# Attention and mixture-of-experts layer: P turned in 32x32 blocks, PV in 32x64 tiles of TensorE

## The reference

```
x = x + attention(layernorm(x));  x = x + ffn(layernorm(x))
q, k, v = y @ W_q + b_q, y @ W_k + b_k, y @ W_v + b_v        # per head, 128 -> 64
P = softmax(causal(q k^T / 8));  z = P v;  out = sum over heads of z W_o, + b_o
```

## Time and profile before

| | us |
|---|---|
| median of 3 runs | 1330.94 (1328.23 to 1332.27) |
| the profiled execution: time | 1327.09 |
| its span | 1325.4 |
| TensorE busy (share) | 1259.4 (95%) |
| VectorE busy | 816.3 (62%) |
| ScalarE busy | 820.3 (62%) |
| GpSimd busy | 302.8 (23%) |

### The profile page before, as it was taken

How to read it: one execution, slowest core, us unless ns; L and a number is a source line. 1 busy time by engine, 2 the same in 40 slices (tenths; PEclk the granted TensorE clock), 3 DMA queues, 4 the chain that set the end, 5 groups by cost and what they waited for, 6 DMA issues and landing times.

```text
span 1325.4 us, 26554 instructions
## 1 busy us (share of the span) xinstructions
PE 1259.4 (95%) x7404; PEld 855.9 (65%) x7404; DVE 816.3 (62%) x2230; ACT 820.3 (62%) x1749; POOL 302.8 (23%) x311
## 2 busy tenths in 40 slices
PE   2899999999999999999999999999999997899995
PEld 1666666667666676676667777666777675445552
DVE  6666666666666666666666666666666676556563
ACT  3756666666666666666666666666666656476664
POOL 3322222222222222222222222222222201012323
PEclk8999999999999999999999999999999998999998
DMA  8866555555555555555555555555555551000000
GB/s 199 207 138 136 130 127 131 131 131 130 128 127 127 127 127 127 127 127 127 127 126 127 127 127 124 127 127 127 127 127 127 127 127 37 9 9 8 16 8 24
DMA packets 78983, 148.68 MB, mean 112 GB/s; under 512 B 41328, under 2 KB 52592, under 8 KB 67056
## 3 DMA queue, kind: packets, MB, share of 16 engines
q1 hardware_dynamic: 78960, 148.41, 49.0%
HBM read 43.21 MB, written 4.46 MB: 36 GB/s over the span
## 4 chain that ended last, share of the span: by engine, by line
PE 80%; DVE 6%; issue 5%; SPq 3%; ACT 2%; DMA 2%; POOL 1%; DVEq 0%; ACTq 0%; POOLq 0%
PE Z L517 19%; PE TB L504 15%; PE SPS L494 10%; PE SPS L495 8%; PE MB L480 8%; PE MB L525 4%; PE MB L485 4%; PE Z L641 2%; PE SPS L633 2%; DVE SSB L849 2%; PE TB L625 1%; PE MB L659 1%; SPq L367 1%; DVE ZN L798 1%; PE SPS L598 1%
## 5 line engine op out<-in xcount | busy, mean ns | idle before, releaser
L849 DVE CUSTOM_DVE_ANT_0 SSB<-SPS,MASK 128x640 f32<-128x640 f32 (+7 forms) x512 | 385.4, 753 | 311.2 <-PE SPS L495 302.7
L1115 ACT ACTIVATE PR<-SSB,NM 128x640 f32<-128x640 f32 (+7 forms) x512 | 394.3, 771 | 109.7 <-DVE NM L849 104.2
L504 PE MATMUL TB<-IDENT,PR 128*128 128x128 f32 x2304 | 349.9, 275 | 17.5 <-ACT PT L780 7.8
L504 PEld LDWEIGHTS TB<-IDENT,PR 128*128 128x128 f32 x2304 | 272.7, 141 | 102.2 <-issue 42.9
L780 ACT ACTIVATE PT<-TB 128x512 f32<-128x512 f32 (+3 forms) x384 | 205.0, 534 | 180.5 <-PE TB L504 180.5
L494 PE MATMUL SPS<-KH,QS 128*128 128x512 f32 (+2 forms) x768 | 313.7, 408 | 2.6 <-DVE NM L849 1.3
L517 PE MATMUL Z<-PT,V 128*64 128x512 f32 (+3 forms) x1536 | 269.3, 492 | 0.0
L495 PE MATMUL SPS<-KL,QS 128*128 128x512 f32 (+2 forms) x768 | 261.5, 348 | 0.0
L395 POOL CAST RH<-RAW 128x512 fp32r<-128x512 f32 x124 | 75.5, 609 | 772.0 <-ACT RAW L1077 769.1
L782 DVE COPY PT<-TB 128x128 f32<-128x128 f32 (+3 forms) x384 | 186.3, 485 | 76.2 <-PE TB L504 76.2
L517 PEld LDWEIGHTS Z<-PT,V 128*64 128x64 f32 x1536 | 101.7, 136 | 141.7 <-issue 132.3
(11 more groups left out here) (157 smaller groups left out, 880.3 us busy)
## 6 DMA issues: line engine op xcount, KB each, us to landing
KH<-RH SPq DMA_DIRECT2D x62, 512.0 KB, 8.6
KL<-RL SPq DMA_DIRECT2D x62, 512.0 KB, 9.1
XTB<-xt_scratch SPq DMA_DIRECT2D x32, 512.0 KB, 4.0
RSB<-rcp_scratch SPq DMA_DIRECT2D x128, 128.0 KB, 2.8
QS<-RH SPq DMA_DIRECT2D x31, 512.0 KB, 4.4
QS<-RL SPq DMA_DIRECT2D x31, 512.0 KB, 6.6
WQK<-in_W_q SPq DMA_DIRECT2D x33, 64.0 KB, 1.9
WQK<-in_W_k SPq DMA_DIRECT2D x33, 64.0 KB, 2.1
```

The source lines that it names most:

```text
L504: last = pe.transpose(TB[idx % 2][:, k * P:(k + 1) * P], PR[n % 4][:, (j0 + k) * P:(j0 + k + 1) * P], IDENT[:, :])
L849: v.tensor_tensor_reduce(out=SSB[n % 2][:, 0:w], in0=SP_[n % 2][:, 0:w], in1=MASK[:, S - w:S], scale=1.0, scalar=BIG, op0=ALU.add, op1=ALU ...
L1115: act.activation(PR[n % 4][:, 0:w], SSB[n % 2][:, 0:w], ACT.Exp, bias=NM[:, col:col + 1], scale=-1.0, accum_out=L[:, col:col + 1]).then_in ...
```

## The change

- TensorE turns nothing any more. VectorE turns the exponentials of a whole unit in 32x32 blocks with one instruction (`dve_turn`), from rings PRS and PRL into PTZ. Inside each block keys and queries are exchanged; which of the four 32-row groups a block lies in stays that of its queries.
- PV is therefore done in tiles of 32 rows by 64 columns: for each key tile kt, each 32-key block j, each row group i (the 32-query blocks) and each head h one matmul, with V's block j in the partitions of group i, and up to 4 x 32 queries streamed. Row group i writes to bank i of ZB. V is stored to DRAM and read back four times into VR, so that each partition group holds all of V.
- PV of both halves is done in the next step: the first half behind unit 3, the second half in one visit behind unit 6.
- TB, Z and MB are now the four banks of ZB, so projections, V, PV and output share them and wait for each other's evacuation.
- RH and RL are gone. GpSimd rounds and subtracts directly into QS, KH and KL, on half of the partitions each (two casts and two subtractions for each quarter), and only K is spread by DMA to the other half: four DMAs of 256 KB.
- ScalarE evacuates V (the bias of V is folded into b_o by `pe_bias`) and copies the output to OT; GpSimd adds OT to X (`add_out`).
- The FFN weights are issued before the sums of step 31.

```diff
+        def turned_block(g, h, kt, j, rows):
+            lo = max(kt - g * TC, 0)
+            key = slice(kt * P + j * TR, kt * P + (j + 1) * TR)
+            step = PT_ROW[g] + h * P
+            c0 = PT_BASE[g] + h * PT_LEAD[g]
+            tiles = PTZ[rows, c0:c0 + TC * step].rearrange("p (r c) -> p r c", c=step)
+            if h == 0:
+                return tiles[:, lo:TC, key]
+            return tiles[:, 0:TC - lo, key][:, ::-1, :]
...
-        def pe_values(pe, it, par, g, j):
...
-            for h in range(2):
-                last = pe.matmul(Z[h * DH:(h + 1) * DH, off:CH], V[par][:, j, h * DH:(h + 1) * DH], PT[g][:, h, j, off:CH],
-                                 start=(j == 0), stop=(j == nj - 1))
+        def pe_values(pe, it, g, blocks):
+            for kt in blocks:
...
+                c0 = g * P + max(kt - g * TC, 0) * TR
+                for j in range(P // TR):
+                    for i in range(P // TR):
+                        rows = slice(i * TR, (i + 1) * TR)
+                        for h in range(2):
+                            last = pe.matmul(ZB[h * DH:(h + 1) * DH, i, c0:(g + 1) * P], VR[rows, j, kt, h * DH:(h + 1) * DH],
+                                             turned_block(g, h, kt, j, rows), start=(kt == 0 and j == 0),
+                                             stop=(kt == (g + 1) * TC - 1 and j == P // TR - 1))
...
+        def spread_v(sp, it, half, par):
+            sp.wait_ge(v_stored[par], (half + 1) * DMA)
+            wait(sp, pv_done[1], it)
+            src = v_dram[par].rearrange("(j k) (t c) -> k j t c", k=TR, c=P)
+            for tiles, landed in ((slice(0, TC), v_early), (slice(TC, QT), v_late)):
+                for i in range(P // TR):
+                    sp.dma_start(VR[i * TR:(i + 1) * TR, :, tiles, :], src[:, :, tiles, :]).then_inc(landed, DMA)
...
+            v.transpose(turned_of(n), exps_of(n)).then_inc(turned, 1)
...
+            gp.tensor_tensor(QS[par][DH:P, h, part], q, q_high.bitcast(F32), ALU.subtract).then_inc(split_done, 1)
+            gp.tensor_tensor(KL[par][DH:P, h, part], k, k_high.bitcast(F32), ALU.subtract).then_inc(split_done, 1)
...
+            scores(2, 3)
+            values(0, 0, 1, 2, 3)
+            scores(4, 5, 6)
+            values(1, 0, 1, 2, 3, 4, 5, 6, 7)
+            scores(7, 8, 9, 10)
...
+            out_of(0)
+            scores(11)
+            qk(2)
+            scores(12)
+            out_of(1)
+            qk(3)
+            scores(13)
+            v_of(0)
+            scores(14)
+            v_of(1)
+            scores(15)
```

More of the change, by code:

```diff
@@ L862, in dve_slot, with dve_step, mask, turn @@
-            if n == 9:
-                dve_reciprocal(v, it, 0, par)
-            if n in (14, 15) and not last:
-                dve_v(v, it + 1, 1 - par, n - 14)
-            if last and n == 0:
-                v.wait_ge(v_evac, STEPS * 2)
+        def dve_step(v, it, half, par, first, last):
+            def mask(n):
+                dve_mask(v, it, par, n)
+            def turn(*units):
+                for n in units:
+                    dve_turn(v, it, n)
+            def turn_back(n):
+                if not first:
+                    dve_turn(v, it - 1, n)
+            def stats(n):
+                if last:
+                    if n == 1:
+                        v.wait_ge(out_evac, (STEPS - HP) * 2 + 1)
+                    f_norm_stats(v, range(3 * n - 3, 3 * n))
+            mask(0)
+            if last:
@@ L880, in dve_slot @@
-            if last and 1 <= n <= 8:
-                if n == 1:
-                    v.wait_ge(out_evac, (STEPS - QT) * 2)
-                f_norm_stats(v, range(3 * n - 3, 3 * n))
+            turn_back(13)
+            mask(1)
+            turn_back(14)
+            mask(2)
+            turn_back(15)
+            if not first:
+                dve_reciprocal(v, it - 1, 1, 1 - par)
+            mask(3)
+            if not first:
+                dve_zn(v, it - 1, 0)
+            stats(1)
+            mask(4)
@@ new lines, in dve_step @@
+            turn(0, 1)
+            stats(2)
+            mask(5)
+            turn(2, 3)
+            stats(3)
+            mask(6)
+            turn(4, 5)
+            stats(4)
+            mask(7)
+            turn(6, 7)
+            dve_reciprocal(v, it, 0, par)
+            stats(5)
+            mask(8)
+            if not first:
+                dve_zn(v, it - 1, 1)
+            stats(6)
+            mask(9)
+            turn(8)
+            stats(7)
+            mask(10)
+            turn(9)
@@ L1142, in _, with turn_of @@
             norm_out(act, 2)
+            act_v(act, 0, 0)
+            act_v(act, 0, 1)
             def body(it, half, par, first, last):
[L1145 to L1146 removed]
+                act_step(act, it, half, par, first, last)
             each_step(act, body)
[L1148 to L1152 removed]
+            def turn_of(k):
                 act.wait_ge(f_turned, k + 1)
```

631 lines of the change are left out of this document (333 added, 298 removed).

## The result

The changed kernel takes 1,780.3 us (median of 4 runs, 1,774.2 to 1,783.0) against 1,329.6 (1,327.6 to 1,332.3) for the kernel before on the same chip: ratio 1.338, 95% interval 1.334 to 1.343. The forecast was 1,283 with a range to 1,430, so it missed on the slow side by 497 us.

A forecast was written before the change was run, and what follows sets the result against it. TensorE was taken to set the 33.8 us step, VectorE and its waits the new 31.9: 59 us saved over 31 steps, ends -4, fetch +15, giving 1,279, as median 1,283 us. Its own range was 1,225 to 1,320, the full range 1,225 to 1,430.

The forecast's parts named there:

- The rest: Costs beside the step: V's transfer nothing, refetching TensorE's loop body 15 us (bounds nothing and 45), ends net -4 us.
- the long one: VectorE waiting for score 7 during the second-half PV visit: about 4.3 us a step.
- at Z: VectorE waiting at the normalisation of Z during the first-half PV visit: 0.8 us a step.
- the small ones: VectorE's further waits at masks 0 and 1 and turns 7 and 11: about 0.6 us each, 2.5 a step.
- rival C: PV is well, but VectorE, fetches or V's transfer cost 1.9 to 5 us more a step: 1,328 to 1,430; chance 0.22.
- A: In PV, serial row-group loads or a floor under each short matmul: 21 us, not 8.4; about 1,660 us; chance 0.10.
- D: Interlock of VectorE and TensorE milder than counted: a step of 29.5 to 30.2 us, 1,200 to 1,220 us; chance 0.04.
- the -4 and +15 of the sum: Whole-run terms: -4 us net at the ends (earlier FFN loads, X's addition), +15 us for refetching TensorE's loop body.
- rival B: In PV only column tiles overlap: PV 31.7 us, a step 55, about 1,990 us; chance 0.06.
- the masks' slope: VectorE's block turns priced at the masks' 1.06 ns a column: 0.71 us each after overlap, sixteen 11.3 us a step.
- TensorE idle with no releaser at each second step (fetch): Sign that the forecast is wrong: at each second step, TensorE idle through instruction fetch; no size given.
- PV waiting for VR: Sign that the forecast is wrong: PV held up by V's transfer, which was costed at nothing.

The follow-up runs named there:

- long-bodied kernel before: The kernel before with six steps instead of two in TensorE's loop body (2,809 instructions instead of 940), same work and order: 1,342.1 us, ratio 1.0095.
- whole-row kernel: The changed kernel with each PV matmul taking all 128 rows, 96 a step instead of 384, most PV arithmetic left out: 1,340.5 us, ratio to before 1.0074.
- 1,564 kernel: The whole-row PV variant with six of twelve key tiles a step split into two blocks of 32-row tiles, body of 1,564 instructions: 1,250.4 us.

## Why the prediction was wrong

**The step that failed** is the term of the sum under "The rest": "TensorE's loop body of two steps grows to about 3,400 instructions ... bounds nothing and 15 x 3 us = 45, I take 15". The fact was right (3,484); the price was wrong in kind. I charged only the jump. The runs show that each packet of 256 instructions also takes 3.4 us, against the 1.7 to 2.0 us in which a burst at full clock uses one up. The page Runtime: NRT & Kernel Launch of the Trainium skill, section Instruction fetch mechanics, calls the cost of passing from one block to the next mostly hidden; the long-bodied kernel before agrees, and the changed one doesn't. Added up, whole rows against all tiles:

- in the visits: 20.1 for 8.7 us a step, x 31 = about 353 us
- at the jumps back: 7.3 less the usual 0.8, x 14 = about 91 us
- sum 444; measured 1,780.3 - 1,340.5 = 440 us. In the forecast: 15.

Not quite all of the 440 is fetch. At the 13.5 ns a record seen above, PV's 768 records would take an estimated 10.4 us a step with all instructions at hand, 1.7 more than the whole rows; that is up to 53 us. No kernel ran all tiles from a body that stays, so the split is an estimate: some 390 to 440 us are the fetches.

The size of the body was also compared with the wrong figure: its 0.22 MB are more than the 0.16 MB of TensorE's queue before, but not "more than all the instructions that the queues fetched", since the other instruction queue moved 0.11 MB.

Bound from above it would have been easy: 3,484 instructions x 15 passes are 204 packets, and the landing of a small transfer, 2.8 us, times 204 is 570 us. I bounded the number of jumps, not that of packets.

**The second error, 62 us.** The step without fetches is 33.9 us, not 31.9. With the 425 us of the first this is 487 of the 497 missed. PV was 8.7 for 8.4. VectorE's work was 24.2 (570.25 of 800 us x 33.9) for 24.3. Its waits were 9.7 for 7.6: the long one 4.61 for 4.3, at Z 1.06 for 0.8, the small ones 4.0 for 2.5. Those I had worked out at full clock; the whole-row kernel's isn't (PE, PEld, DVE, ACT, POOL, clock):

```profile
300.00:304.00 4.00, 2.83 (x6) 1.44 (x7) 2.27 (x8) 3.33 (x8) 2.55 (x3) 0.70 0.21 38
...
332.00:336.00 4.00, 2.21 (x12) 1.49 (x11) 3.73 (x8) 3.47 (x7) 3.58 (x5) 0.96 1.02 203
336.00:340.00 4.00, 4.00 (x10) 2.07 (x10) 2.10 (x4) 2.16 (x6) 2.22 (x3) 0.61 0.50 99
```

TensorE is busy 2.21 of 4 us where the step changes, and then runs at a mean of 0.61, so mostly at the lower level of 1.2 GHz; the two halves of the Q/K projections there start 1.01 and 0.85 us apart, and 0.43 at 2.4 GHz. The kernel before stays at 1.00 in its steady part. How the 1.5 us divide between clock and waits I didn't separate. Of rival C ("VectorE, the fetches or V's transfer cost 1.9 to 5 us more a step") the fetches and V's transfer came about, the fetches at well over twice its dearest price; VectorE's own work came out as forecast, its waits grew by 2.1 us a step. The times given for A, C and D add their steps to 1,330 and leave out the -4 and +15 of the sum, some 11 us; no reading here hangs on that.

**What was right.** All eight tiles run side by side: starts in eights, 7 ns between neighbours, 13.7 ns a record at 128 columns and full clock, which is an eighth of the full-array price. So rival B fell, and A at its full price of 27 ns a record. But about half of A's floor is there: the first-half visit above takes 13.5 ns a record although most of its tiles are narrower. The estimated 10.4 us for PV is 2.0 above the 8.4 forecast, and just at the price where A was to decide; behind the fetch it stayed hidden. The whole-row kernel's 8.7 us don't speak for the eight tiles, since it runs only two side by side. The overhead for each matmul that the page TensorEngine Tiling (Array Packing) of the Trainium skill gives in its section Instruction Overhead (an estimated 19 us a step) isn't seen at that size: by its figure it would be an estimated 25 ns a record, where 13.5 were measured. That the visits do take 20.1 us is a coincidence, as the 1,564 kernel shows. The block turns, forecast from the masks' slope, came out right at both ends, and don't scatter under GpSimd's load:

```profile
L856 DVE STREAM_TRANSPOSE PTZ<-PRL 128x1024 f32<-128x1024 f32 x64 | 79.3, 1240 | 0.0
...
L856 DVE STREAM_TRANSPOSE PTZ<-PRS 128x128 f32<-128x128 f32 x64 | 16.1, 289 | 0.0
```

1,024 columns in 1.24 us as forecast, 128 in 0.29 (0.211 + 96 x 0.00106 = 0.31). "TensorE idle with no releaser at each second step (fetch)" was named as the sign of an error, and was there; that it would stand inside PV wasn't foreseen. "PV waiting for VR" doesn't show: V's transfer was on time and did most of its harm at another place.

## What to carry to other kernels

Count instructions as well as columns. Where a change multiplies the instructions of a loop, compare the body with the longest that was seen to stay on the engine (here 1,564), and the densest stretch with the rate of fetch (here 256 in 3.4 us): above both, in these runs, the fetch was the engine's time, whatever the array could do. An "issue" wait that repeats every 256 instructions, beside a grown instruction queue, is its mark. If such a body can't be avoided, deal the short instructions out between long ones, write the loop out, and keep large transfers away from the jump.

## What the runs showed of the hardware

- A TensorE loop body of 1,564 instructions stayed, one of 1,756 was fetched again on every pass; nothing between was run. The Trainium skill, page Runtime: NRT & Kernel Launch, section Instruction fetch mechanics, gives TensorE room for 2,048; by these runs a loop gets less.
- Away from a jump, instruction packets (256 instructions, 16 KB) came 3.2 us apart at the closest in any run, and mostly 3.4 or more, though each took only 0.9 to 1.4 us. In the 124 stops inside PV the packet (1.0 us), the time from its end to the restart (1.4) and the time from there to the next packet (1.1) follow each other.
- Tiled float32 matmuls of 32x64 with nothing to fetch took 13.5 to 14.9 ns a record; eight of 128 columns started within 110 ns, but narrow ones weren't faster in proportion.
- A jump to code that isn't there cost 2.6 us a step in the kernel before with the long body. From the last start ahead of the jump to the first behind it, the changed kernel took 2.7 us without V's transfers, and 7.3 with V's loads filling the DMA engines (0.8 where the code is there): instruction packets came late behind the data.
- The granted clock was no measure of the loss: 0.754 and 0.847 gave the same time within 0.6%, since the engine was waiting for instructions either way.
